# Context in a second layout, and a new order in VectorE's early units of the third stage

## The reference

```python
# x: (16,128,512), ctx_512: (16,128,128)
x = x + tanh(g_xattn[0]) * L0_xattn(layernorm(x), ctx_512, ...)   # stage 1
x = x + tanh(g_ffn[0])   * L0_ffn(layernorm(x), ...)              # stage 2
x = x + tanh(g_xattn[1]) * L1_xattn(layernorm(x), ctx_512, ...)   # stage 3
x = x + tanh(g_ffn[1])   * L1_ffn(layernorm(x), ...)              # stage 4

def L1_xattn(q, latent_kv, Wq, Wkv_expand, Wout):   # 16 heads of 32
    qp = q @ Wq.T
    k, v = split(latent_kv @ Wkv_expand.T, 2, axis=-1)
    scores = einsum('bhqd,bhkd->bhqk', qh, kh) / sqrt(32)
    attn = softmax(where(causal, scores, -inf), axis=-1)
    return einsum('bhqk,bhkd->bhqd', attn, vh) @ Wout.T
```

## Time and profile before

| | us |
|---|---|
| median of 3 runs | 1345.37 (1344.8 to 1349.57) |
| the profiled execution | 1344.79 |
| its span, first to last instruction | 1343.0 |
| PE busy | 1321.1 (98%) |
| DVE busy | 932.6 (69%) |
| ACT busy | 517.6 (39%) |
| POOL busy | 404.2 (30%) |

### The profile page before, as it was taken

The page is one execution under the profiler, slowest core; times in us unless marked ns, Lnnn a source line. Parts: engine busy times, 40 slices in busy tenths (PEclk is TensorE's granted clock), DMA queues, the critical chain, the costliest instruction groups (busy, mean ns, idle before and its releaser), DMA issues.

```text
span 1343.0 us, 20310 instructions
## 1 busy us (share of the span) xinstructions
PE 1321.1 (98%) x7404; PEld 1069.2 (80%) x7404; DVE 932.6 (69%) x1805; ACT 517.6 (39%) x1569; POOL 404.2 (30%) x461
## 2 busy tenths in 40 slices
PE   7999999999999999999999999999998899999998
PEld 6888888888887788778887888788876687778877
DVE  5765676675775868775778667776888787846533
ACT  3544445454564331231123111411127777732210
POOL 4212323231256252101120111113426866630000
PEclk9999999999999999999999999999999999999999
DMA  8755454444572232210221012112324556555431
GB/s 298 230 169 160 147 168 142 157 149 134 186 224 74 83 87 71 83 40 16 64 83 53 18 40 89 42 48 67 104 92 145 182 181 205 173 197 156 149 110 55
DMA packets 131655, 163.51 MB, mean 122 GB/s; under 512 B 15436, under 2 KB 85196, under 8 KB 131556
## 3 DMA queue, kind: packets, MB, share of 16 engines
q1 hardware_dynamic: 131556, 162.22, 38.0%
HBM read 109.74 MB, written 52.43 MB: 121 GB/s over the span
## 4 chain that ended last, share of the span: by engine, by line
PE 91%; DVE 4%; ACT 3%; DMA 1%; issue 0%; POOL 0%; SPq 0%; DVEq 0%; ACTq 0%; POOLq 0%
PE bank L118 89%; PE bank L121 2%; ACT P L124 2%; DVE st L152 1%; DVE STG L130 0%; DVE sm L146 0%; DVE AH L130 0%; DVE AR L130 0%; DMA XR<-in_x_dram 0%; ACT AR L124 0%; ACT STG L124 0%; DMA STG<-in_WqT_dram 0%; ACT bank L124 0%; DVE AH L127 0%; DVE PTV L127 0%
## 5 line engine op out<-in xcount | busy, mean ns | idle before, releaser
L118 PE MATMUL bank<-XT,AR 128*128 128x512 f32 x1152 | 280.1, 393 | 0.1
L118 PE MATMUL bank<-AR 128*128 128x512 f32 x1056 | 258.5, 395 | 1.7 <-DVE AR L130 1.7
L118 PEld LDWEIGHTS bank<-XT,AR 128*128 128x128 f32 x1152 | 213.9, 188 | 48.2 <-issue 1.5
L124 ACT ACTIVATE STG<-bank,b1c 128x512 f32<-128x512 f32 x128 | 88.3, 690 | 387.1 <-PE bank L118 313.7
L118 PEld LDWEIGHTS bank<-AR 128*128 128x128 f32 x1056 | 194.2, 188 | 47.8 <-issue 2.8
L118 PE MATMUL bank<-AR,CT 128*128 128x512 f32 x768 | 191.3, 392 | 0.0
L118 PE MATMUL bank<-AR,AH 128*128 128x512 f32 x768 | 185.9, 390 | 0.0
L127 DVE CAST AH<-STG 128x512 fp32r<-128x512 f32 x192 | 91.1, 475 | 112.6 <-PE bank L118 98.7
L118 PEld LDWEIGHTS bank<-AR,AH 128*128 128x128 f32 x768 | 143.6, 188 | 30.6 <-issue 1.1
L118 PEld LDWEIGHTS bank<-AR,CT 128*128 128x128 f32 x768 | 140.2, 188 | 27.0 <-issue 0.4
L127 POOL CAST BA<-STG 128x256 fp32r<-128x256 f32 x64 | 31.3, 489 | 396.1 <-PE bank L118 241.0
(11 more groups left out here) (143 smaller groups left out, 1818.9 us busy)
## 6 DMA issues: line engine op xcount, KB each, us to landing
XR<-scr SPq DMA_DIRECT2D x64, 256.0 KB, 3.0
pscr<-PYZ SPq DMA_DIRECT2D x30, 512.0 KB, 2.9
PYZ<-pscr SPq DMA_DIRECT2D x120, 128.0 KB, 2.9
XR<-in_x_dram SPq DMA_DIRECT2D x32, 256.0 KB, 4.1
XR<-lscr SPq DMA_DIRECT2D x128, 64.0 KB, 2.0
scr<-XR SPq DMA_DIRECT2D x32, 256.0 KB, 2.1
pscr<-STG SPq DMA_DIRECT2D x16, 512.0 KB, 2.6
PTV<-pscr SPq DMA_DIRECT2D x64, 128.0 KB, 2.8
```

The source lines that it names most:

```text
L118: return self.e.matmul(o, w, x, start=start, stop=stop, skip_group_check=True) if self.e else Nothing()
L124: return self.e.activation(o, x, func, **kw) if self.e else Nothing()
```

## The change

1. Context: a second copy of the input, `ctxT`, holds the context transposed (the host lays it out so, as it does the other inputs). `cx_load` loads it in place of the token-major copy; PE's `cx_turn` goes (4 transposes each for m = 0 to 3); ACT and DVE (`cx_split`) split the tile straight from `XR`; K and V wait for the split (`cx_ok`). For m = 1 to 3 the ring of banks has one take less.
2. DVE, units 3 to 7: `turn_p3(u-2)` stands ahead of `largest(u-1)` and not behind `q3_out(u)`.
3. DVE, unit 2: K's copy stands ahead of `turn_p3(0)` and not behind the reciprocals and it.
4. Rows: the layernorm tile (2, 1, 3) is normalised by DVE behind K's copy of unit 3, and not by POOL.
5. V of group 1 (unit 6): DVE copies blocks 0 and 1 ahead of `av3`'s low part and 2 and 3 behind it; before, DVE copied 0 and 2 behind it and ACT 1 and 3.
6. The loads and splits of stage 4's weights start in unit 4, and not in unit 2.

```diff
         def normed_by_pool(ph, m, tb):
-            return (ph, m) in ((2, 1), (2, 2), (2, 3), (3, 0)) and (ph, m, tb) not in ((2, 1, 0), (2, 1, 1))
+            return (ph, m) in ((2, 1), (2, 2), (2, 3), (3, 0)) and (ph, m, tb) not in ((2, 1, 0), (2, 1, 1), (2, 1, 3))
...
-        w4_step = {u: [u - 2] for u in range(2, 14)}
+        w4_step = {u: [u - 4] for u in range(4, 16)}
...
-            def cx_turn(m, ring):
-                src = xr_ap("cx", m)
-                k = ps.take(("cxT", m), ring.next())
-                pe.wait_ge(*ps.free(("cxT", m)))
-                pe.wait_ge(*xr_ld("cx", m))
-                for b in range(4):
-                    s = slice(128 * b, 128 * b + 128)
-                    ins = pe.transpose(k[:, s], src[:, s], ident[:, :])
-                ins.then_inc(*ps.fill(("cxT", m)))
...
-                    pe.wait_ge(*ps.drained(("cxT", m)))
+                    pe.wait_ge(*cx_ok[m])
...
-            def cx_turn(m):
-                ac.wait_ge(*ps.full(("cxT", m)))
+            def cx_split(m):
+                ac.wait_ge(*xr_ld("cx", m))
                 ac.wait_ge(*(ps.full(("k3", 4 * m - 1)) if m else cm_ok[63]))
                 if m:
                     ac.wait_ge(*ps.full(("v3", m - 1, 3)))
-                hi_of(("cxT", m), CXT[:, 0, :], ps.ap(("cxT", m))[:, :])
+                hi_of(("cxT", m), CXT[:, 0, :], xr_ap("cx", m))
...
-                if values and k_first(u):
-                    v3(m, 1)
-                    v3(m, 3)
...
-            def cx_turn(m):
-                lo_of(("cxT", m), CXT[:, 1, :], ps.ap(("cxT", m))[:, :], CXT[:, 0, :]).then_inc(*ps.drain(("cxT", m), on_dve))
+            def cx_split(m):
+                lo_of(("cxT", m), CXT[:, 1, :], xr_ap("cx", m), CXT[:, 0, :]).then_inc(*cx_ok.mark(m))
...
             for u in range(18):
                 m, g = divmod(u, 4)
+                if 3 <= u < 8:
+                    turn_p3(u - 2)
                 if 1 <= u <= 16:
                     for j in range(4):
                         largest(u - 1, j)
...
                 if u == 2:
                     ln_norm(2, 1, 0)
                     ln_norm(2, 1, 1)
-                if u >= 2:
+                    k3(2)
+                if u == 2 or u >= 8:
                     turn_p3(u - 2)
...
-                if 1 < u < 16:
+                if 2 < u < 16:
                     k3(u)
+                if u == 3:
+                    ln_norm(2, 1, 3)
+                if u > 4 and g == 2 and k_first(u):
+                    v3(m, (0, 1))
                 if k_first(u):
                     av3(u - 3)
                 if u > 4 and g == 2 and k_first(u):
-                    v3(m)
+                    v3(m, (2, 3))
...
-                e.dma(xr_ap("cx", m).rearrange("p (b d) -> p b d", b=4),
-                      i["ctx"][512 * m:512 * m + 512, :].rearrange("(b l) d -> l b d", b=4)).then_inc(*d_xr[xr_at["cx", m]].mark(("cx", m)))
+                e.dma(xr_ap("cx", m), i["ctxT"][:, 512 * m:512 * m + 512]).then_inc(*d_xr[xr_at["cx", m]].mark(("cx", m)))
```

More of the change, by code:

```diff
@@ L366, in build @@
         vy_ok, vz_ok, py_ok, pz_ok, ly_ok, lz_ok = kinds(on_dve, "vy_ok vz_ok py_ok pz_ok ly_ok lz_ok")
-        (p3y_ok,) = kinds(on_dve, "p3y_ok")
+        p3y_ok, cx_ok = kinds(on_dve, "p3y_ok cx_ok")
         c_mh, c_sel, rs_ok, kvc_rd, kvr_ok, kvl_ok = kinds(on_pool, "c_mh c_sel rs_ok kvc_rd kvr_ok kvl_ok")
@@ L433, in xr_free @@
             if old[0] == "cx":
-                return ps.full(("cxT", old[1]))
+                return cx_ok[old[1]]
             return t_xr[xr_at[key]][old]
@@ L932, in tensor @@
                     else:
-                        cx_turn(0, Ring((7,)))
                         stCm(F, range(4))
@@ L1086, in tensor @@
                         ln_turn(*after3(m), tb, ring3.next())
-                if u < 16 and g == 3 and m + 1 < NM:
-                    cx_turn(m + 1, ring3)
                 if u < 16 and g == 3:
@@ L1399, in scalar @@
                     if not more:
-                        cx_turn(0)
+                        cx_split(0)
                     if more:
@@ L1491, in scalar @@
                 if u < 16 and g == 3 and m + 1 < NM:
-                    cx_turn(m + 1)
+                    cx_split(m + 1)
                 if u < 16 and g == 3:
@@ L1901, in vector, with v3 @@
                     if not more:
-                        cx_turn(0)
+                        cx_split(0)
                         tail_x(m, (2, 3))
-            def v3(m):
-                for b in (0, 2) if m else range(4):
+            def v3(m, blocks):
+                for b in blocks:
                     e.wait_ge(*ps.full(("v3", m, b)))
@@ L1972, in vector @@
                     k3(1)
-                    v3(0)
+                    v3(0, range(4))
                 if 1 <= u <= 16:
@@ L1982, in vector @@
                 if u > 4 and g == 2 and not k_first(u):
-                    v3(m)
-                if 1 < u < 16:
+                    v3(m, (0, 2))
+                if 2 < u < 16:
                     k3(u)
+                if u == 3:
+                    ln_norm(2, 1, 3)
+                if u > 4 and g == 2 and k_first(u):
+                    v3(m, (0, 1))
                 if k_first(u):
@@ L2268, in gpsimd @@
                     for tb in tiles3(u)[g]:
-                        ln_norm(*after3(m), tb)
+                        if normed_by_pool(*after3(m), tb):
+                            ln_norm(*after3(m), tb)
                 if u == 1:
@@ L2661 @@
     a["ctx"] = C(I["ctx_512"].reshape(NT, 128))
+    a["ctxT"] = C(I["ctx_512"].reshape(NT, 128).T)
     a["g4"] = rows(np.stack([I["g_xattn"][0], I["g_ffn"][0], I["g_xattn"][1], I["g_ffn"][1]]))
```

## The result

The changed kernel takes 1349.35 us (median of 11 runs, 1347.76 to 1350.92), the kernel before beside it 1344.8 us. The ratio is 1.0026, 95% interval 1.0017 to 1.0034: 3.5 us slower, between 2.3 and 4.6 us. Forecast were +2.3 us and 1347.7 us, inside the band of 0.5% about no change; the time lies in the range.

The account below looks back on a forecast made before the run. PE, 98% busy, was taken as the bound, with a DVE and ACT loop on the chain from 1011 to 1067 us; -0.5 + 3.4 - 0.4 - 0.2 = +2.3 us gave 1347.7 us, range 1340.5 to 1351.5 us.

Parts of the forecast that it names:

- The chain runs through DVE and ACT from 1011 to 1067 us, and what stands ahead of `largest` is paid: Units 3 to 7: P's turn of 1.2 us ahead of `largest` lengthens the DVE and ACT loop, +3.4 us in all.
- The +1.0 in unit 4: Unit 4: DVE's 1.42 us idle ahead of `largest` pays part of the turn, so the delay's sum is +1.0 us.
- Context, -0.5 at the start, -0.4 and -0.2 later: Dropping the context's transposes saves 0.5 us at the stage's start, 0.4 in unit 7 and 0.2 in unit 11.
- m = 1, in unit 3: Context's second block: transposes stand on PE while DVE and ACT are late, so dropping them gains nothing.
- K's copy, 0: Unit 2: PE gains some 0.7 us for the scores, but DVE reaches `largest` no earlier; 0 us.
- Tile and weights, 0: POOL is ready 4 us earlier, DVE normalises the tile in idle time (0.5 us), weight loads have spare units; 0 us.
- V in unit 6 and the turn in unit 7, 0: V's new copy order gives 0 (between -0.6 and +0.6); unit 7's turn delays DVE 1 us, covered by PE's long unit.
- PE's mask and scores are late by the 3.4 us: Unit 7: PE's work is late by the loop's summed 3.4 us, as tiles turned last in unit 6 await DVE's banks.
- Rival 1: The gaps close and PE gains from K's copy, the late tile and 16 transposes: about -4 us, 1341.5 us; chance 0.16.
- Rival 2: The turn ahead of `largest` is free, scores come late, only the transposes count: -1.1 us, 1344.3 us; chance 0.12.
- Rival 3: The turn waits for POOL's scaling and delays `largest` in up to five units: 1352.7 us with 1 us each; chance 0.06.
- Rival 4: Context's split with two SBUF inputs meets POOL in units 3, 7, 11: up to 3 us more, 1350.7 us; chance 0.08.

Follow-up runs that it names:

- e1: Changed kernel with P's turn put back behind `q3_out` in units 3 to 7; 1342.44 us, ratio 0.9983 to the kernel before.
- e2: Kernel before with only P's turn moved ahead of `largest` in units 3 to 7; 1350.97 us, ratio 1.0044.
- e7: As e1, but with P's turn ahead of `largest` in units 4 and 5 alone; 1345.24 us, ratio 0.9998.
- e9: Changed kernel with P's turn in units 3 to 7 between `largest` of head 1 and of head 2; 1342.07 us, ratio 0.9979.
- e4: Changed kernel with V of unit 6 copied as before (DVE blocks 0 and 2, ACT 1 and 3); 1348.02 us, ratio 1.002.
- e3: Kernel before with only the context loaded in a second layout, without transposes, and split from `XR`; 1342.28 us, ratio 0.9982.
- e5: Changed kernel with PE making the product for block 2 of V in unit 6 four times; 1347.46 us, ratio 1.0007.
- e6: As e1, with DVE's layernorm statistics of units 4 to 6 moved ahead of the low part of `av3`; 1343.19 us, ratio 0.9975.
- e8: As e6, PE making two blocks of V in unit 6 ahead of `av3`, DVE copying all four ahead of the low part; 1343.98 us, ratio 0.9986.
- e11: As e8, with P's turn between `largest` of head 1 and of head 2 in units 3 to 7; 1341.87 us, ratio 0.9978.
- e10: As e6, with P's turn between `largest` of head 1 and of head 2 in units 3 to 7; 1341.19 us, ratio 0.9972.
- e12: As e6, with P's turn ahead of `largest` in unit 4 alone; 1341.49 us, ratio 0.9974.

## Why the prediction was right

The number is nearer than its terms. By the ratios of e1 the turn costs 5.8 us (forecast 3.4) and the rest of the edit brings 2.3 us (forecast 1.1): both were put too small, and since they pull in opposite directions, +2.3 came out near +3.5. The direction and the loop were understood; that much of the closeness is luck.

- **The chain runs through DVE and ACT from 1011 to 1067 us, and what stands ahead of `largest` is paid**: shown, by e1, e2, e7 and e9. Against the entry, the first `largest` of units 3 to 6 came later than before by 1.20, 0.90, 2.06 and 3.25 us (1028.16 against 1026.75 us and so on, less 0.21); forecast were 1.2, 1.0, 2.2 and 3.4. The +1.0 in unit 4 has a wrong reason: the scores that DVE waited for there come behind the low part and are late with it. With 1.2 us more ahead of the low part they would let `largest` start 1.2 us late, at 1038.92 us, and the idle time would pay nothing (an estimate, from 1037.72 us). That it is 0.90 comes of the 0.67 us of the context's edit, which brings the scores forward.
- **Context, -0.5 at the start, -0.4 and -0.2 later**: unit 7 and unit 11 give -0.3 to -0.5 and -0.3, as forecast. From PE's last matmuls ahead of the transposes to the first scores of the stage it is 11.27 us and was 11.89 (996.06 to 1007.33 us, 995.22 to 1007.11): -0.6, as forecast. The entry was no earlier in the profile (+0.22) because PE reached that place late: it had waited 0.8 us for POOL's split of a weight near the end of stage 2, 0.6 more than before. That wait lies outside the change, and e4's entry was 1.2 us earlier than the kernel before. The term that was mis-sized is m = 1, in unit 3, put at nothing: the recorded text saw that the ring has one take less and wrote that "either way it waits for DVE's low part", but one block of transposes waits where two did, and that is 0.67 us. With it and 0.4 us in unit 12 the places come to some 2.4 us, which is e3's ratio; in the changed kernel only 0.3 of the 0.67 us counts, as the turn then ends later than the scores come, and unit 12 gave nothing back (+0.25).
- **K's copy, 0**: PE gained 0.60 us in unit 2 and DVE nothing, as forecast.
- **Tile and weights, 0**: PE's wait for POOL's tile became one of 1.6 us for DVE's. DVE's normalisation took 1.23 us, not 0.5: it started while POOL scaled P (1031.37 us, 2.04 us for two), and ended behind the second of these. It cost nothing, for it lies in DVE's idle time.
- **V in unit 6 and the turn in unit 7, 0**: here the sum was too small. PE's scores of unit 7 came 4.8 us later than before (less the entry's 0.2), where 3.4 were forecast and DVE's first `largest` of unit 6 was 3.25 us late. The step that failed is "PE's mask and scores are late by the 3.4 us": it held PE's own work at its old durations. After a wait of 2.24 us PE ran at 1.2 GHz for 3 to 4 us, which made the other 1.6 us; in e5, at full clock, the same scores are 3.2 us late (the table's units 2 to 6 against before), which is the loop's share and nothing else.
- **Rival 1** (the gaps close) fell in the changed kernel: the gaps moved. **Rival 2** (the turn is free in front) holds in unit 4 in part, where e7 found 0.34 us. **Rival 3** did not occur: the turn follows the operation ahead of it at once, and no DVE wait is put down to POOL. **Rival 4** cost 0.3 us once, in unit 7; the low parts of units 3 and 11 took 0.68 us.

## What to carry to other kernels

When the chain of waits runs in a loop over two engines, ask of every instruction of the slower list whether it stands ahead of the one that releases the other engine, or behind it; the turn of 1.2 us in each of five units cost 5.8 us in one place and nothing two instructions later. The waits named in the list of PE's waits were symptoms here: closing two of them moved the time to others. When a ring of banks has one take less, work out which instructions no longer wait, even if the last one still does. And an edit that lets TensorE stand still longer should be priced with the lower clock behind the gap, not with the gap alone.

## What the runs showed of the hardware

- The granted clock fell to 0.50 (1.2 GHz) behind PE's waits of 2.2 us in the changed kernel, e2, e4 and e6 (in e2 behind one of 1.28 us too), and matmuls of 389 ns took 628 ns or more. It fell behind waits of 2.08 us in e8 and 1.99 in e11, but not behind 1.98 us in e8's unit 6 and 1.81 in e10. Behind waits of 1.65 us it fell in e3 and not in the kernel before, with the same work ahead of them. The kernel before has executions with a mean clock below 1.00 as well (2 of the 27 beside e1 to e4, 10 of the 29 beside e5 to e8, 3 of the 28 beside e9 to e12). What decides in such a case stays open.
- DVE's low part of the context, now with two SBUF inputs, took 0.97 us in unit 7, beside an operation of POOL (1083.26 us, 1.04 us), and 0.68 us in unit 3 without one. DVE and POOL of the changed kernel:

```profile
1036.94 0.68 DVE L130 TENSOR_TENSOR AR<-XR,AR 128x512 fp32r<-128x512 f32 x1
...
1083.87 0.97 DVE L130 TENSOR_TENSOR AR<-XR,AR 128x512 fp32r<-128x512 f32 x1
```
```profile
1083.26 1.04 POOL L130 TENSOR_TENSOR P<-P,sm 128x512 f32<-128x512 f32 x1 [1.77 <-DVE sm L149]
```

The Trainium skill, "SBUF — State Buffer", section "Who interferes with whom", has this as an exclusive lock on a shared pair of ports. The trace agrees in kind: DVE's operation ran 0.3 us long and ended at 1084.84 us, where a full block until POOL's end (1084.30) and its usual 0.68 us would give 1084.98.
